# Context loads moved to GpSimd, token statistics ahead of the small weights, and the out weight quantized inside unit 0

## The reference

```
x = x + xattn(layernorm(x), ctx)           # 8 x 512 x 512, ctx 8 x 1601 x 512
  q = qdq(x) @ qdq(wq).T + bq              # qdq: int8 rounding, one scale a row
  k, v = split(ctx @ wkv.T + bkv)
  o = softmax(q k^T / sqrt(32)) v          # 16 heads of 32
  out = qdq(o) @ qdq(wp).T + bp
x = x + experts(layernorm(x))              # 8 experts, the best 2 for each token
```

## Time and profile before

| what | us |
|---|---|
| median of 3 runs (2104.82 to 2109.83) | 2106.23 |
| the profiled execution | 2110.97 |
| its span, first to last instruction | 2109.3 |
| start, until the first exponential | 93.2 |
| attention from there to its last scores | 93.2 to 1612.7 |

### The profile page before, as it was taken

One profiled execution on the slowest core, in us unless ns is written; L12 is line 12 of the kernel. 1 busy time (PEld: TensorE's weight loads), 2 busy tenths in 40 slices (PEclk: granted clock), 3 DMA queues, 4 the chain that ended last, 5 costly groups with the idle time before them and its releaser, 6 DMA issues. The chain is left out here.

```text
span 2109.3 us, 60295 instructions
## 1 busy us (share of the span) xinstructions
PE 1812.7 (86%) x24774; PEld 1256.2 (60%) x24774; DVE 1765.7 (84%) x2319; ACT 1390.2 (66%) x2017; POOL 874.5 (41%) x727
## 2 busy tenths in 40 slices
PE   2699898989999998999999899989995216999996
PEld 1577675766667676767666676767773103555553
DVE  4599898989999998999999999999996495666665
ACT  4378676878778786888787787878876332333322
POOL 2122421643273247226522732471234202676766
PEclk9899999999999999999999999999997557999998
DMA  4312232332333223324332332232220254567785
GB/s 160 111 33 77 81 93 48 101 89 90 78 95 100 53 79 104 92 58 111 94 90 78 95 96 57 79 104 76 71 56 27 86 159 146 183 197 224 239 263 185
DMA packets 151922, 224.31 MB, mean 106 GB/s; under 512 B 33188, under 2 KB 86436, under 8 KB 151648
## 3 DMA queue, kind: packets, MB, share of 16 engines
q1 hardware_dynamic: 127760, 164.27, 27.1%
q0 software_dynamic: 22016, 55.60, 8.6%
q10 hardware_dynamic: 1872, 0.55, 0.1%
HBM read 130.32 MB, written 70.79 MB: 95 GB/s over the span
## 5 line engine op out<-in xcount | busy, mean ns | idle before, releaser
L823 DVE TENSOR_TENSOR a_p_low<-a_p 128x1024 f16<-128x1024 f32 (+1 forms) x896 | 1114.2, 1270 | 107.3 <-ACT a_p L662 99.3
L662 ACT ACTIVATE a_p<-ps_s 128x1024 f32<-128x1024 f32 (+1 forms) x896 | 858.9, 965 | 269.5 <-PE ps_s L468 259.9
L468 PE MATMUL ps_s<-a_q_stack,a_k_stack 96*128 96x512 f16 (+1 forms) x1664 | 512.3, 383 | 1.3 <-ACT a_p L662 1.1
L585 PE MATMUL ps_o<-a_v,a_p 128*128 128x65 f16 (+1 forms) x6656 | 447.7, 194 | 61.2 <-issue 27.8
L585 PE MATMUL ps_o<-a_v,a_p_low 128*128 128x65 f16 (+1 forms) x6656 | 447.6, 194 | 0.0
L585 PEld LDWEIGHTS ps_o<-a_v,a_p 128*128 128x128 bf16 (+1 forms) x6656 | 354.8, 98 | 150.8 <-issue 55.7
L505 PEld LDWEIGHTS ps_p<-wkv,a_ctx 128*128 128x128 f16 x4992 | 320.0, 98 | 142.3 <-DVE a_v L838 20.6
L505 PE MATMUL ps_p<-wkv,a_ctx 128*128 128x128 f16 x4992 | 366.0, 220 | 26.5 <-DVE a_v L838 11.3
L487 PE MATMUL ps_p<-a_ctx,wkv 128*128 128x384 f16 (+2 forms) x1536 | 354.4, 338 | 18.1 <-DVE a_k_parts L829 9.6
L585 PEld LDWEIGHTS ps_o<-a_v,a_p_low 128*128 128x128 f16 (+1 forms) x6656 | 318.0, 98 | 0.0
L384 POOL TENSOR_TENSOR a_ctx<-a_ctx_raw,a_ctx 128x384 f16<-128x384 f32 (+2 forms) x124 | 231.0, 1880 | 95.7 <-ACT a_ctx L703 95.3
(11 more groups left out here) (230 smaller groups left out, 2073.9 us busy)
## 6 DMA issues: line engine op xcount, KB each, us to landing
a_k_stack<-a_k_parts SPq DMA_DIRECT2D x378, 80.0 KB, 2.1
d_ys<-f_y SPq DMA_DIRECT2D x71, 256.0 KB
a_ctx_raw<-in_ctx_dram SPq DMA_DIRECT2D x64, 192.0 KB, 2.7
a_q_stack<-d_q_t SPq DMA_DIRECT2D x96, 128.0 KB, 3.4
a_xm<-in_x_dram SPq DMA_DIRECT2D x8, 1024.0 KB, 5.8
d_q_t<-a_q_parts SPq DMA_DIRECT2D x32, 256.0 KB, 2.7
d_q_full<-a_xm SPq DMA_DIRECT2D x32, 256.0 KB, 2.8
a_x_in<-in_x_dram SPq DMA_DIRECT2D x32, 256.0 KB, 3.2
```

Of the source, the lines that this page charges most:

```text
L468: mm = pe.matmul(t["ps_s"][s % 2][0:r, n * N:(n + 1) * N], t["k_stack"][v % 2][0:TERMS * DH, j, kt * P:kt * P + r], t["q_stack"][v % 2][0: ...
L585: mm = pe.matmul(t["ps_o"][:, q * VC:(q + 1) * VC], part[0:r, n * N + q * P:n * N + (q + 1) * P], val, start=(g == 0 and n == 0 and low == ...
L662: act.activation(t["p"][s % NP][0:r, 0:len(tiles) * N], t["ps_s"][s % 2][0:r, 0:len(tiles) * N], ACT.Exp, scale=float(DH) ** -0.5 / WSCALE ...
L823: dve.tensor_tensor(t["p_low"][s % NP][0:r, 0:n], full, high, ALU.subtract).then_inc(lows, 1)
```

## The change

POOL issues every context load after the first four, right behind its own low part of the piece four before; SP issues none. POOL also takes the low parts of the first four pieces. The gate weight joins `biases_in`, the work `small` goes from slot 5 of the start to slot 24, and the rows bv_row and bp_row are loaded by ACT only after `split_high(1)`. The inverse root of batch 0 is taken by DVE. In the start, casts of ranges 2 and 3 come at slots 24 and 30, k(0,3) before v(0,1), query projections 1 to 3 after the values. SP loads wp right behind the key/value weight, and wp is quantized in steps in slots 7 to 31 of attention (unit 0 and the first slots of unit 1). For later batches the centring, the maxima and the scales of the queries come three slots earlier, and the context casts are spread over seven slots a range. The value half of the key/value weight has a semaphore of its own.

```diff
-FIRST_ORDER = [("k", 0), ("k", 1), ("k", 2), ("v", 0), ("v", 1), ("k", 3), ("v", 2), ("v", 3)]
-FIRST_JOBS = [28, 31, 34, 37, 39, 43, 45, 47]
-FIRST_QUERIES = [29, 36, 38, 40]
-FIRST_CONTEXT = [10, 16, 26, 40]
+FIRST_ORDER = [("k", 0), ("k", 1), ("k", 2), ("v", 0), ("k", 3), ("v", 1), ("v", 2), ("v", 3)]
+FIRST_JOBS = [28, 31, 34, 37, 39, 42, 44, 46]
+FIRST_QUERIES = [29, 48, 50, 52]
+FIRST_CONTEXT = [10, 16, 24, 30]
...
-            self.put("q_scales", b, 0, at + (34 if main else 20))
+            self.put("q_scales", b, 0, at + (31 if main else 20))
...
-                self.put("q_centre", b, m, at + (24 + 2 * m if main else 13))
-                self.put("q_amax", b, m, at + (27 + 2 * m if main else 18))
+                self.put("q_centre", b, m, at + (21 + 2 * m if main else 13))
+                self.put("q_amax", b, m, at + (24 + 2 * m if main else 18))
...
-                    at = (NBLK * b - 2) * SLOTS + (12, 19, 25, 31)[r] + (0, 2, 3, 5)[c] if b else FIRST + FIRST_CONTEXT[r]
+                    at = (NBLK * b - 2) * SLOTS + 13 + 7 * r + (0, 2, 3, 5)[c] if b else FIRST + FIRST_CONTEXT[r]
...
-        for name, x in (("small", 5), ...
-                        ("wp_scale", 48), ("wp_ints", 50), ("wp_row", 50)):
+        for name, x in (("small", 24), ...
+        for c in range(CC):
+            self.put("wp_amax", 0, c, 7 + c)
+            self.put("wp_scaled", 0, c, 13 + c)
+        for name, x in (("wp_inverse", 12), ("wp_round", 18), ("wp_row", 22)):
+            self.put(name, 0, 0, x)
         for half in range(2):
-            self.put("wp_turn", 0, half, FIRST + 52 + half)
+            self.put("wp_ints", 0, half, 20 + half)
+            self.put("wp_turn", 0, half, 26 + 4 * half)
...
+        w_q[1] = [t["xn_parts"][half][:, :, :].bitcast(BF16) for half in range(2)]
...
@@ SP
                 for b, n in plan.at("context_load", s):
-                    if b or n >= CC:
-                        load_context(sp, b, n, ctx_in)
                     if b == 0 and n == 2 * CC - 1:
                         sp.dma_start(wp_raw[:, :, :], ...).then_inc(wp_in, 16)
...
@@ ACT
-            act.dma_start(t["gate_raw"]...).then_inc(rows_in, 16)
-            act.dma_start(t["bv_row"]...).then_inc(rows_in, 16)
-            act.dma_start(t["bp_row"]...).then_inc(rows_in, 16)
+            act.dma_start(t["gate_raw"]...).then_inc(biases_in, 16)
...
                 for _ in plan.at("kv_high_v", s):
                     split_high(1)
+                    act.dma_start(t["bv_row"]...).then_inc(rows_in, 16)
+                    act.dma_start(t["bp_row"]...).then_inc(rows_in, 16)
...
@@ DVE
-                for b, n in plan.at("context", s):
-                    if b == 0 and n < CC:
-                        context_low(dve, b, n)
...
+                    guess = guess_inverse(...)
+                    if b >= 1:
+                        guess.then_inc(q_measured, 1)
+                    else:
+                        done(guess)
+                        done(dve.tensor_scalar(t["q_nmean"][:, :], t["q_mv"][:, :, 0], -1.0, None, ALU.mult))
+                        for n in range(3):
+                            done(dve.tensor_tensor(r, rstd, rstd, ALU.mult))
+                            done(dve.tensor_tensor(r, r, t["q_var"][:, :], ALU.mult))
+                            done(dve.tensor_scalar(r, r, -0.5, 1.5, ALU.mult, ALU.add))
+                            last = dve.tensor_tensor(rstd, rstd, r, ALU.mult)
+                            ...
+                        last.then_inc(q_first_rooted, 1)
...
@@ POOL
                 for b, n in plan.at("context", s):
-                    if b >= 1 or n >= CC:
-                        context_low(pool, b, n)
+                    context_low(pool, b, n)
+                    ahead = b * 4 * CC + n + NRAW
+                    if ahead < B * 4 * CC:
+                        load_context(pool, ahead // (4 * CC), ahead % (4 * CC), ctx_in)
                 for b, _ in plan.at("q_norm", s):
+                    if b == 0:
+                        continue
```

More of the change, by code:

```diff
@@ L410, in _ @@
                                 sp.dma_start(kv_raw[c][:, part * C:(part + 1) * C],
-                                             t["wkv_t"][c * P:(c + 1) * P, part * C:(part + 1) * C]).then_inc(kv_in, 16)
+                                             t["wkv_t"][c * P:(c + 1) * P, part * C:(part + 1) * C]).then_inc((kv_in, kv_in_v)[part], 16)
                 for u, h in plan.at("stack", s):
@@ L706, in split_high @@
                 for c in range(CC):
-                    act.wait_ge(kv_in, 16 * (part * CC + c + 1))
+                    act.wait_ge((kv_in, kv_in_v)[part], 16 * CC)
                     act.mul(t["wkv"][:, 0, c, part * C:(part + 1) * C], kv_raw[c][:, part * C:(part + 1) * C],
@@ L727, in _ @@
                     split_high(1)
+                    act.dma_start(t["bv_row"][:, :], t["bkv"][C:2 * C][None, :].to_broadcast([P, C])).then_inc(rows_in, 16)
+                    act.dma_start(t["bp_row"][:, :], t["bp"][None, :].to_broadcast([P, C])).then_inc(rows_in, 16)
                 for _ in plan.at("wq_ints", s):
                     weight_ints(0, wq_raw, wq_rounded, wq_ints)
-                for _ in plan.at("wp_ints", s):
-                    weight_ints(1, wp_raw, wp_rounded, wp_ints)
+                for _, half in plan.at("wp_ints", s):
+                    act.wait_ge(wp_rounded, 1)
+                    act.activation(w_q[1][half], wp_raw[:, 2 * half:2 * half + 2, :], ACT.Identity,
+                                   bias=t["unround"][:, 0:1]).then_inc(wp_ints, 1)
                 if s > LAG and (s - LAG) % GROUPS == 0 and s <= LAST + LAG:
@@ L797, in _ @@
                     act.wait_ge(centred, i + 1)
+                    if i < 2:
+                        wait_matmuls(act, ("wp_turn", 0, 1))
                     if i >= 2:
@@ L866, in weight_scale @@
                                              ALU.min)
-                if n == 0:
-                    last = dve.tensor_copy(t["sq"][:, :], scale)
-                else:
-                    for c in range(CC):
-                        last = dve.tensor_scalar(wp_diag[:, c, :], k["id32"][:, :], t["w_scale"][:, n, c:c + 1], None,
-                                                 ALU.mult)
-                done(last)
+                done(dve.tensor_copy(t["sq"][:, :], scale))
                 dve.tensor_scalar(raw[:, :, :], raw[:, :, :], -QMAX, ROUND, ALU.max, ALU.add).then_inc(rounded, 1)
@@ L908, in _ @@
                     dve.tensor_copy(t["wq_t"][:, :, :], wq_ps).then_inc(wq_copied, 1)
-                for _ in plan.at("wp_scale", s):
-                    weight_scale(1, wp_raw, wp_in, wp_rounded)
+                for _, c in plan.at("wp_amax", s):
+                    dve.wait_ge(wp_in, 16)
+                    done(dve.tensor_reduce(t["w_amax"][:, 1, c:c + 1], wp_raw[:, c, :], AX.X, ALU.max,
+                                           apply_absolute_value=True))
+                for _ in plan.at("wp_inverse", s):
+                    done(dve.tensor_scalar(t["w_scale"][:, 1, :], t["w_amax"][:, 1, :], 1.0 / QMAX, 1e-8, ALU.mult,
+                                           ALU.max))
+                    done(dve.reciprocal(t["w_inv"][:, 1, :], t["w_scale"][:, 1, :]))
+                for _, c in plan.at("wp_scaled", s):
+                    dve.tensor_scalar(wp_diag[:, c, :], k["id32"][:, :], t["w_scale"][:, 1, c:c + 1], None, ALU.mult)
+                    done(dve.tensor_scalar(wp_raw[:, c, :], wp_raw[:, c, :], t["w_inv"][:, 1, c:c + 1], QMAX, ALU.mult,
+                                           ALU.min))
+                for _ in plan.at("wp_round", s):
+                    dve.tensor_scalar(wp_raw[:, :, :], wp_raw[:, :, :], -QMAX, ROUND, ALU.max,
+                                      ALU.add).then_inc(wp_rounded, 1)
                 for _, half in plan.at("wp_copy", s):
@@ L941, in _ @@
                         dve.wait_ge(q_centred, b * QT)
-                    guess_inverse(t["q_mv"][:, :, 1], t["q_var"][:, :], t["q_rstd"][:, :]).then_inc(q_measured, 1)
+                    guess = guess_inverse(t["q_mv"][:, :, 1], t["q_var"][:, :], t["q_rstd"][:, :])
+                    if b >= 1:
+                        guess.then_inc(q_measured, 1)
+                    else:
+                        done(guess)
+                        done(dve.tensor_scalar(t["q_nmean"][:, :], t["q_mv"][:, :, 0], -1.0, None, ALU.mult))
+                        r, rstd = t["tmp"][:, :], t["q_rstd"][:, :]
+                        for n in range(3):
[3 more added lines that the diff above has]
+                            last = dve.tensor_tensor(rstd, rstd, r, ALU.mult)
+                            if n < 2:
+                                done(last)
+                        last.then_inc(q_first_rooted, 1)
                 for b, m in plan.at("q_amax", s):
```

26 lines of the change are left out of this document (14 added, 12 removed).

## The result

The changed kernel takes 2071.76 us (median of 4, 2068.79 to 2072.7); the kernel before, run beside it, 2108.03. The ratio is 0.9824, interval 0.9803 to 0.9846. Faster was given 0.85, and 2068 was predicted, with 8 chances in 10 for 2052 to 2098. The profiled execution took 2072.02 us with a span of 2070.3, against 2109.3 before.

A forecast was written before the change was run, and what follows sets the result against it. In attention DVE is nearly always at work; recoverable are the start and DVE's holes. Gains of 19 (start) and 28 (boundaries with centring) less 9 (out weight) make 38 off the median 2106.2: 2068 us, 8 in 10 for 2052 to 2098.

The forecast's parts named there:

- Term 1: Start: earlier loads, casts and root bring the first exponential from 93.20 to 74.3 us; gain 19 us, 14 to 23.
- the credit for the order: Start: k0.3 no longer waits 8.02 us for range 3, and query projections 1 to 3 stand behind the values.
- Term 2: Unit 0 of attention: DVE's work on the out weight moves into slots 7 to 31, unhidden; loss 9 us, 8 to 11.
- Term 3: Seven batch boundaries: context loads no longer stand behind SP's key stacks, so DVE's holes close; 35 us before the discount.
- the discount of 4: Boundaries: 4 us taken off the 35 for new small waits of ACT on POOL.
- POOL's room: Boundaries: 18 us free for 16 issues, so an issue may take 1.1 us before POOL sets the pace; 0.57 taken.
- Term 3b: Queries' centring three slots earlier: ACT waits for POOL's root in batch 2 and unit 0, later batches not; loss 3, 0 to 7.
- (a): Rival, boundaries: the hole has another owner, ACT waits as long on POOL, the start alone pays; 2096 us, chance 0.15.
- (b): Rival, start: it gives nothing net, boundaries alone pay; 2078 us, or 2092 with half the boundaries; chance 0.13.
- (d): Rival, loads: they still land late because POOL issues them behind its own backlog; 2100 us, chance 0.03.
- (c): Rival, boundaries: POOL sets the pace and the kernel is slower, 2138 us, deciding from about 1.3 us an issue; chance 0.09.

The follow-up runs named there:

- the experiment: The changed kernel with the out weight's quantization moved back as one piece to the end of the start: 2112.28 us, ratio 0.9834 to the kernel before.
- the kernel with the hole: The changed kernel with the vector part of the out weight's quantization at slot 28 of the start, where DVE waits for PE: 2063.88 us, ratio 0.9796.

## Why the prediction was right, and where its steps were off

**Term 1, the start:** gain 19 predicted, 16.8 measured, inside 14 to 23. The casts of range 1 ended at 24.8 (23.5 predicted), k0.0 started at 41.0 (37.5), v0.0 at 56.1 (52.6), v0.3 ended at 68.9 (66.5), and from there to the exponential it took 7.6 (7.8). Of the 3.5 us missing at k0.0, 2.8 go to one sentence: that the root is ready 9 us after x lands or sooner "because the 13 small steps run on DVE without the handover to POOL". It was ready 11.1 us after (8.44 to 19.56), because DVE's steps were stretched by POOL's new work beside them. With four of POOL's subtractions taken away, k0.0 started at 38.2. The other step that failed is the credit for the order: "k0.3 no longer waits 8.02 us" is true, but with the old order the first exponential is no later. There v0.3 ended at 72.4, 10.2 us earlier than before, and the exponential stood 0.5 us behind it in place of 10.6. So the gain is that of the out weight's leaving and of the earlier loads, casts and root together. No run takes these last three apart.

**Term 2, the out weight:** loss 9 predicted (8 to 11), and by the experiment it is 8.1: 6.9 in unit 0 and 1.2 in unit 1. Unit 0 grew by 10.6, more than the out weight costs, but unit 1 became 2.7 shorter; with the queries late the two are 48.4 and 46.0 in place of 50.5 and 43.3. The earlier queries move work from the one to the other and cost nothing there.

**Term 3, the boundaries:** 35 predicted without the discount of 4, and the seven units became 33.8 us shorter. The size came from what DVE idled there, and it held: DVE's idle time fell by 31.6 us, its busy time by 2.4. The discount, for new small waits of ACT on POOL, shows in no run. The cause was told too simply. Of the 34 us POOL's loads alone bring 22, the even cast slots alone 22. The prediction gave all to the loads and didn't price the slots; the loads do close the holes, but DVE's own steps get longer if the slots stay uneven. POOL's room was mis-sized: 18 us free at a boundary were spread over 16 loads as 0.5 us each without cost, yet that much more per load cost 3.3 us. Left out were POOL's 0.30 us wait for its own subtraction before each load, a root of 8.5 us in place of 5 (413.96 to 422.42 at the second boundary), and that DVE gets slower: three quarters of that 3.3 us is DVE being busy longer. And a sum over a whole boundary hides the bursts: POOL waits 67.8 us for casts in the changed kernel, while in other stretches it works without a gap.

**Term 3b, the centring:** loss 3 predicted (0 to 7), 5 to 6 measured, in part by luck. The two waits came where they were expected (5.1 us together), but units 0 and 1 lost nothing by them and units 4 and 5 lost 1 to 2 us. The rest, 4 to 6 us, lies in units 9, 13, 17, 21 and 25, where the prediction had said "later batches not".

**The sum:** 16.8 for the start, 7.9 lost in units 0 and 1, 33.8 at the boundaries and 3.9 lost in all other units make 38.8, against 19 - 9 + 28 = 38. None of the three numbers of the forecast is off by more than 2.2 us, and the errors nearly cancel, which is luck. The 38.8 us lie between two profiled executions; between the medians it is 36.3, since the profiled execution of the kernel before was 2.9 us above its median. Of the rivals, (a) needed ACT to wait for POOL instead; its only new waits for POOL are the two for the root. In (b) the start would have given nothing. (d) needed late loads, and ACT waits for none. (c) is real and starts nearer than its 1.3 us, but at 0.56 us an issue the gain is far larger than its cost.

## What to carry to other kernels

When a change moves an issue and shifts slots too, test each alone: here either half brought two thirds of the gain. An engine's room counted over a whole stage is not room: count it in the burst, with the wait before each issue and with the engine beside it slowed. Compare busy and idle time of the engine that sets the pace: a stage can get longer with little new idle time, because its steps got longer. Work that must leave one place goes first into a hole that the trace shows, as the out weight did in the kernel with the hole, and only then among other work.

## What the runs showed of the hardware

**DVE stood still beside POOL.** In the changed kernel's start DVE's steps of 128x4 elements took 1.60, 1.59 and 1.60 us where others took 0.16. Each of the three began during one of POOL's direct issues and ended when POOL's next subtraction did: 12.91 + 1.60 = 14.51 against 13.31 + 1.17 = 14.48. The weight's scaling (L880) took 3.41 us for four, and 1.68 in the kernel where DVE did the first subtractions itself. The Trainium skill ("SBUF — State Buffer", SBUF: two separate sides) says that of a GpSimd operation and a DVE operation with two SBUF inputs or in a 2-port mode the one that starts first holds the shared ports and the other stands still for the whole of it. The whole stop agrees. Who was first doesn't, by the records: DVE's step, 0.16 us long when alone, is recorded from 12.91, the subtraction that it outlasted only from 13.31. Of POOL only an issue, recorded from 12.75, was under way at 12.91. An issue alone didn't stop DVE in the kernel where DVE did the first subtractions: there four issues ran from 15.43 for 2.34 us beside its four subtractions of 128x512, which took 2.49 us in all. What held DVE in those 0.4 us stays open.

**An issue by POOL costs more than its row.** 0.56 us for the instruction and 0.30 before it, 33.1 us over 108 loads. An issue of half a load took 0.53 and one of a quarter 0.50: the size hardly matters.

**A hole costs PE its clock.** The granted clock was 0.53 in the 5 us from the end of a hole of 9.95 us, 0.50 (the lower level, 1.2 GHz) in the 5 us from just before the end of one of 2.70, 0.71 in the 5 us that hold most of one of 2.13, and 1.00 at the third boundary after the change, where there was none.
